# A graph layer with experts on one core: TensorE loads a tile's loop bounds among the expert products of the step before

## The reference

```python
x = x + (segment_sum((layernorm(x) @ W)[dst] * edge_weight, src) + bias)
xn = layernorm(x) * gamma + beta
w = softmax over the top 2 of (xn @ Wr + br), zero for the other experts
x = x + sum_e w[:, e] * (gelu(xn @ W1[e] + b1[e]) @ W2[e] + b2[e])
```

## Time and profile before

| | us |
|---|---|
| median of 3 runs | 3774.95 |
| lowest and highest | 3774.81, 3778.23 |
| profiled execution | 3771.83 |
| its span, first to last instruction | 3770.1 |
| TensorE busy | 3237.5 (86%) |
| VectorE busy | 2486.9 (66%) |
| GpSimd busy | 2402.3 (64%) |
| ScalarE busy | 1339.0 (36%) |

### The profile page before, as it was taken

The page is one execution under the profiler, slowest core; times in us unless marked ns, Lnnn a source line. Parts: engine busy times, 40 slices in busy tenths (PEclk is TensorE's granted clock), DMA queues, the critical chain, the costliest instruction groups (busy, mean ns, idle before and its releaser), DMA issues. The chain is left out here.

```text
span 3770.1 us, 77968 instructions
## 1 busy us (share of the span) xinstructions
PE 3237.5 (86%) x21468; PEld 2119.4 (56%) x21468; DVE 2486.9 (66%) x6355; ACT 1339.0 (36%) x2814; POOL 2402.3 (64%) x2251
## 2 busy tenths in 40 slices
PE   6679777644799999999999999999999999999997
PEld 3445444422455555555555555555555555567886
DVE  9699655534666676667666676666676667655664
ACT  1353766630122222223222222222222222255664
POOL 1151388877766766666667667676667676674555
PEclk8899888876899999999999999999999999999999
DMA  4342010103333333333334333333333333454554
GB/s 151 98 131 71 27 26 25 26 14 89 110 104 105 107 103 107 104 107 100 110 94 117 95 111 105 102 104 107 101 105 109 102 108 103 122 157 99 90 88 67
DMA packets 258290, 358.36 MB, mean 95 GB/s; under 512 B 86661, under 2 KB 199370, under 8 KB 257994
## 3 DMA queue, kind: packets, MB, share of 16 engines
q0 software_dynamic: 108032, 247.79, 25.2%
q1 hardware_dynamic: 106968, 64.44, 6.4%
q10 hardware_dynamic: 42996, 42.43, 3.5%
HBM read 290.79 MB, written 63.57 MB: 94 GB/s over the span
## 5 line engine op out<-in xcount | busy, mean ns | idle before, releaser
L804 POOL DMA_INDIRECT area<-h_table,listed x1664 | 1672.3, 1005 | 748.8 <-issue 482.4
L1901 PE MATMUL twin<-area 128*128 x2800 | 1024.1, 410 | 174.5 <-issue 148.8
L1903 PE MATMUL twin<-area 128*128 x2800 | 811.1, 290 | 0.0
L977 ACT ACTIVATE area<-twin,b_t 128x512 f32<-128x512 f32 x208 | 142.9, 687 | 1340.9 <-PE twin L1954 793.8
L1901 PEld LDWEIGHTS twin<-area 128*128 x2800 | 289.9, 104 | 575.6 <-issue 336.3
L1434 DVE TENSOR_TENSOR area<-area,listed 128x1024 f16 x700 | 453.2, 689 | 114.5 <-DVE area L1426 98.0
L772 POOL DMA_INDIRECT edge_list<-area,didx x256 | 326.6, 1276 | 76.2 <-issue 76.2
L1423 DVE TENSOR_SCALAR rel<-listed,tile_no 128x8 f16 x350 | 83.4, 238 | 418.2 <-issue 365.4
L1903 PEld LDWEIGHTS twin<-area 128*128 x2800 | 289.6, 103 | 60.3 <-issue 0.4
L1971 PE MATMUL bank<-w2h,area 128*128 128x256 f16 x1664 | 304.7, 273 | 0.0
L831 POOL DMA_INDIRECT out_dram<-area,put_row x108 | 185.2, 1715 | 164.2 <-DMA out_dram<-area,put_row 73.0
(11 more groups left out here) (381 smaller groups left out, 6190.7 us busy)
## 6 DMA issues: line engine op xcount, KB each, us to landing
area<-h_table,listed POOLq DMA_INDIRECT x1664
area<-in_x_dram SPq DMA_DIRECT2D x194, 128.0 KB, 2.2
area<-zs SPq DMA_DIRECT2D x54, 260.0 KB, 2.8
h_table<-area SPq DMA_DIRECT2D x97, 128.0 KB, 1.7
xt<-in_x_dram ACTq DMA_DIRECT2D x97, 128.0 KB
area<-in_L_ffn_W_dram ACTq DMA_DIRECT2D x16, 512.0 KB, 4.0
out_dram<-area ACTq DMA_DIRECT2D x12, 512.0 KB
out_dram<-area ACTq DMA_DIRECT2D x46, 128.0 KB, 2.8
```

What stands on the lines that cost most here:

```text
L804: pool.indirect_dma_start(out=stage[:, (k % RU) * UNIT + 2 * D * c:(k % RU) * UNIT + 2 * D * (c + 1)], out_offset=None, in_=h_table[:, :], ...
L1901: nc.tensor.matmul(psA[:, :], target[:, ds(at, P, 2)], stage[:, ds(rows, 2 * D)], start=False, stop=False)
L1903: last = nc.tensor.matmul(psA[:, 0:D], target[:, ds(at + TGT // 2, P, 2)], stage[:, ds(rows, D)], start=False, stop=False)
```

## The change

A new function `bound(b, k)` loads one of the three bounds of tile `b`. `chunks` gets them as arguments and loads nothing. `hidden(i, then_tile)` loads one bound of the next tile behind each of its first three quarters and returns the three. In the steps that have no expert (`t` from 0 to 3) they are loaded where `hidden` would stand, and those of tile 0 in front of the loop. The number of loads, the matmuls, their order and the waits stay the same, and so do the other engines' programs.

```diff
+            def bound(b, k):
+                if k == 0:
+                    return pe.value_load(lo_i[0:1, ds(b, 1)], min_val=0, max_val=NU)
+                if k == 1:
+                    return pe.value_load(end_i[0:1, ds(b, 1)], min_val=1, max_val=NU + 1)
+                return pe.value_load(off_i[0:1, ds(b, 1)], min_val=0, max_val=2 * NT)
+
-            def chunks(b):
+            def chunks(b, first, end, off):
                 reached(pe, s_x1, b, gate=False)
                 nc.tensor.matmul(psA[:, :], one_h[:, :], bias_hl[:, :], start=True, stop=False)
-                first = pe.value_load(lo_i[0:1, ds(b, 1)], min_val=0, max_val=NU)
-                end = pe.value_load(end_i[0:1, ds(b, 1)], min_val=1, max_val=NU + 1)
-                off = pe.value_load(off_i[0:1, ds(b, 1)], min_val=0, max_val=2 * NT)
                 with pe.Fori(first, end) as u:
...
-            def hidden(i):
+            def hidden(i, then_tile):
                 c, e = i // NE, i % NE
+                found = []
...
                     last.then_inc(s_w1, 1)
+                    if then_tile < NT and m < 3:
+                        found.append(bound(then_tile, m))
+                return found
...
+            visits_of = [bound(0, k) for k in range(3)]
             for t in range(NEX + SB + 1):
                 i = t - SB
                 if t < NT:
-                    chunks(t)
+                    chunks(t, *visits_of)
...
                 if 0 <= i < NEX:
-                    hidden(i)
+                    visits_of = hidden(i, t + 1)
+                elif t + 1 < NT:
+                    visits_of = [bound(t + 1, k) for k in range(3)]
```

## The result

The changed kernel takes 3661.99 us (median of 4 runs, 3658.69 to 3665.44), the kernel before took 3775.34 beside it: a ratio of 0.9697, 95% interval [0.9683, 0.9711]. It is 113 us faster; 94 were predicted. The profiled execution took 3664.54 us (span 3662.8), 107.3 less than the one of before.

What follows compares the result with a forecast made beforehand. The prediction took TensorE, held by its loads before the visits, as the bound and VectorE's waiting as the limit: 136.9 − 16 − 10 − 17 = 94 us gained, 3681 us beside the median, range 3630 to 3735.

Steps and rivals of the forecast that it cites:

- the one floor: After the change VectorE ends each step, so its 136.9 us of waiting limit how far the steps can shrink.
- The chain of 1.9 us: Three loads in front of TensorE's visits: 1.9 us of sequencer time in each of 92 tiles, 175 us removed.
- The price of an issue: Sequencer time per first-layer matmul, 0.10 to 0.163 us; six and a load take 1.24 or 1.62 against 1.29.
- the step: The prediction's working from VectorE's 136.9 us of waiting, less 16, 10 and 17, to a gain of 94 us.
- the rival of loads that still cost TensorE: Moved loads open gaps in the first layer, 1.0 us a tile: gain only 8 to 75 us, chance 0.17.
- the slower one: First-layer loads wait for earlier matmuls to enter the array, each a 0.64 us gap: up to 3850 us, chance 0.10.
- The ring: GpSimd's gathers come 2.2 us late at tile 27, once in some eight tiles: 17 us deducted.
- VectorE's double waits: In 29 steps two second-layer waits total 2.4 us, more than TensorE gives: 16 us deducted.
- the clock before the transposes: TensorE idles before the transposes and its clock can fall: 0.3 us in a third of the steps, 10 us deducted.
- VectorE's 136.9 us: VectorE's waits for TensorE in the second layer and for the ranks, taken as the most the steps can shrink.

Runs made afterwards that it cites:

- both floors eased: Changed kernel with VectorE's bounds loaded a step earlier and seven of eight gathers a unit behind the first eight units: 3562.03 us, ratio 0.9431.
- the gathers alone: Kernel before with seven of each unit's eight gathers behind the first eight units, loads left in place: 3771.53 us, ratio 0.999.
- the ring eased: Changed kernel with seven of each unit's eight gathers behind the first eight units, VectorE's program untouched: 3619.48 us, ratio 0.9589.
- the first filled kernel: Kernel before with seven one-row matmuls of zeros between the bias matmul and the three loads: 3798.71 us, ratio 1.0068.
- the run with twelve loads: Changed kernel with each moved load done four times in the first layer: 3892.31 us, ratio 1.0307.
- the run with a third of the chain: Changed kernel with only `off` loaded in the first layer, `lo` and `end` still in front of the loop: 3701.08 us, ratio 0.981.

## Why the prediction was right, and where its terms were off

The mechanism held, but for the one floor (below). The idle time before the visits fell to 23.7 us (under 50 was predicted), the first visit came 0.32 us behind the bias (0.25), VectorE's wait for the second layer fell from 132.7 to 30.6 (under 50), GpSimd's wait for room fell by 115.9 while the time fell by 107 to 113, and TensorE got both new waits.

**The chain of 1.9 us was right.** All of it comes back where nothing else is in the way. With both floors eased the kernel takes 213 us less than the one of before (3775.42 to 3562.03): 92 × 1.9 = 175 and 34 for the clock are 209, and the gathers alone are worth 4 at most. TensorE's timelines, added up from tile 6 to 96, say the same in another way. With both floors eased, 120 us go between the logits and the first visit, 86 in the visits (the clock's 34 and 52 of the chain) and 2 elsewhere.

In the changed kernel the same 120 us go in front of the visits, but only 33 in the visits, which now hold the waits for gathers (45.7 us more). From the first layer to the next logits, 46 us are added: the waits before the transposes (30.2 more) and at L1997 (7.4 more) and 8 that no run takes apart. That leaves the 107 us by which the profiled execution is shorter. This is one engine's path, so it shows where the time went and not which engine made it.

**The price of an issue (0.10 to 0.163 us) was too high**, both ends. It was taken from the visits, whose matmuls have their addresses worked out in registers; with fixed addresses six of them add 0.02, so one costs about 0.003. The conclusion, that the quarter covers the load, was right with much more room than the step gave it, and the rival of loads that still cost TensorE fell with it; so did the slower one, since the loads ran before the matmuls in front of them had gone into the array.

**The ring was mis-sized: 17 us predicted, 42.5 measured** by easing it. The step let the four tiles from 23 to 26 shrink by 4.8 us and put 2.2 us too much on tile 27. TensorE's bias matmuls of tiles 23 and 27, before and after, show 94.1 and 87.6 us, so 6.5 had gone:

```profile
1440.62 0.39 PE L1891 MATMUL twin<-bias_hl,one_h 1*128 1x512 f16 x1
...
1534.72 0.39 PE L1891 MATMUL twin<-bias_hl,one_h 1*128 1x512 f16 x1
```

```profile
1417.84 0.39 PE L1898 MATMUL twin<-bias_hl,one_h 1*128 1x512 f16 x1
...
1505.45 0.39 PE L1898 MATMUL twin<-bias_hl,one_h 1*128 1x512 f16 x1
...
1534.19 0.39 PE L1898 MATMUL twin<-bias_hl,one_h 1*128 1x512 f16 x1
```

Tile 27 then waits 3.56 us, and what follows runs at half clock: the tile takes 28.7 us, where it took 26.0. The step charged a shorter wait, in two of three rounds, and no clock behind it. The other two deductions, 16 us for VectorE's double waits and 10 for the clock before the transposes, are hardly seen: with the ring eased, 8.9 us of VectorE's wait for the second layer are left, and the granted clock fell three times in the stage. (By its own figures, 2.4 us against the 1.9 that TensorE gives, the first would be 29 × 0.5 = 14.5 and not 16; that changes little.) That the three together make 43, as the ring alone does, is chance.

**VectorE's 136.9 us were not the most that the steps could shrink.** With VectorE's program untouched and the ring eased, the kernel was 154 us faster than before (3773.19 to 3619.48). The step counted three groups of VectorE's waits and left out those for the places of its targets (16.2 us before, 7.3 after) and some smaller ones:

```profile
DVE area L1434 <- PE twin L1903: 16.2, 48, 0.7
```

All its waits for other engines' work are 166 us in the kernel before and 25 with the ring eased, which is 142 of the 154; the rest is not taken apart. So the number came out better than its terms. Without the ring, the step's sum is 136.9 − 16 − 10 = 111, where 154 was measured: 43 too little, 17 of it by the start and 26 by the two deductions. The ring's term is 25 too small and hides more than half of that. That 94 lies only 19 below 113 is in part luck. The wider claim, that VectorE is *the* floor, is wrong: there are two floors close together, the ring and VectorE, and what frees one runs into the other.

## What to carry to other kernels

A load of a value into a register costs little where a sequencer has lead, and its full length where the array has run dry: look for the program's stretch with the longest work per issued instruction, and put loads there, as many as its length covers. Before you take a wait away, list every engine's waits in the same stretch, all groups and not the largest three; the next floor is the engine whose waits are the smallest against what you take out, and there may be two. Filler tells a gap's own cost from the clock's only where the clock then stays up and the filler delays nothing itself, so read the granted clock of such a run first, and then when the work behind the filler starts.

## What the runs showed of the hardware

- Matmuls with one row of weights (1*128) kept the array busy without a gap and the granted clock still fell to its lower level behind them. TensorE's timeline of the first filled kernel, the end of the seven and the visit behind them, whose matmuls grow from 0.38 to 0.6 us:

```profile
1497.83 1.67 PE L1893 MATMUL twin<-bias_hl,zero_h 1*128 1x512 f16 x7
1499.43 0.39 PE L1903 MATMUL twin<-area 128*128 x1
...
1500.37 0.63 PE L1903 MATMUL twin<-area 128*128 x1
```

  With matmuls of 128 rows, in front of the bias, the clock was 1.00 over the stage. The one-row matmuls also multiply zeros and stand behind the bias, so the runs don't show which of these differences matters.
- The three gaps a tile of up to 1.3 us inside the first layer, in the run with twelve loads, left the clock at 1.00 over the stage; the gap of 1.37 us behind the logits and the bias let it fall in the kernel before. In the run with a third of the chain, the granted clock fell in 25 stretches of the stage, and at 23 of these the longest gap near by was 0.7 to 0.8 us, in front of a tile's first visit. So the length of a gap alone doesn't say whether the clock falls.

```profile
985.00:3390.00 2405.00, 2072.05 (x12999) 1255.01 (x12996) 1566.25 (x4344) 607.88 (x1065) 1580.73 (x1568) 1.00 0.35 100
```

- The sequencer went through six matmuls of fixed addresses in about 0.02 us (0.66 us from load to load with them, 0.64 without), and began a load into a register 0.4 us before the first of them was in the array. A visit's sixteen matmuls with addresses from registers set a pace of 3.06 us where it had no lead.
